# Turning the second norm's rows by DMA from SBUF in place of TensorE transposes, in a one-core decoder kernel

## The chip, the cores and the metric

The kernel runs on one core of a Trainium2 chip, in one launch. The metric is the device time of the run in microseconds (us), the median of several runs. Before the change it is 846.45 us (three runs, 845.71 to 847.24).

## The reference

A decoder layer with three parts, each followed by a layer norm over 512 features; 8 batches of 128 tokens.

```python
x = _layernorm(x + _L0_attn_ref(x, ...))                   # causal self-attention, 32 heads of 16
x = _layernorm(x + _L0_xattn_ref(x, ctx, ctx, mask, ...))  # 32 query heads, 8 key heads of 128, rope
x = _layernorm(x + _L0_ffn_ref(x, ...))                    # gate, up, down; 4-bit weights
# the third part, which reads the output of the second norm:
gate = x2 @ Wg
up = x2 @ Wu
inter = gate * jax.nn.sigmoid(gate) * up
out = (inter @ Wd).astype(jnp.float16)
```

Its inner size is 1376, padded here to 11 tiles of 128. The change concerns the way from the second norm to `x2 @ Wg` and `x2 @ Wu`.

## The kernel before

All 1024 tokens stay in SBUF. `res` holds the running rows: 128 tokens on the partitions, eight batches of 512 features. A product over the features needs the activations turned, with features on the partitions; these are `aTh` and `aTl`, each 128 x 4 x 1024 in fp16. Every fp32 value is split into a high and a low fp16 part, and each product is three matmuls: high by high, low by high, high by low. ScalarE makes the high part (`split_hi`), VectorE subtracts it to get the low part (`split_lo`).

`cTh` and `cTl` hold the turned cross-attention context in the same way. Their last reader is the value projection of the last block of keys and values; after it their room is free until parts of the inner activations are written there.

The program is a row of steps t. From step T0 = 70 on, each step v = t - 70 handles one tile of cross-attention (one batch, four heads), and END = 134. Each engine executes its own list in the order written, and waits on semaphores. For tile v: TensorE makes the scores in step v, VectorE their maximum (`nmax`), ScalarE the exponentials (`prob`) and their sums, VectorE the inverse sums (`rden`), GpSimd the normalised probabilities, ScalarE and GpSimd their two fp16 parts (`pn`). SyncE's DMA queue turns them into `pT` (line 469), and TensorE uses `pT` in step v+2 (`weigh`) and multiplies by the output weights in step v+3 (`merge`). ScalarE and VectorE split the weighed values into `o2h` and `o2l` between these two. "Fills" are projections and turns that TensorE does beside the tiles, by the table of `fill_plan`.

The second norm of batch b is applied when the last head group of that batch is done: in step 127 + b for batches 0 to 3, in step 131 + b for batches 4 to 7 (`APPLY_SLOT`). TensorE then turns the batch: four fp32 transposes of 128 x 128 into a PSUM bank, from which `turned_hi` and `turned_lo` (or `late_turned_hi` and `late_turned_lo`) write `aTh` and `aTl`. Batches 0 to 3 are fills in steps 129, 129, 130 and 131; batches 4 to 7 are turned by `late_turn` in steps 136 to 139.

The first consumer is `gate_or_up`: gate and up for the tiles i = 0 to 3 of the inner size and batches 0 to 3. The first of these (gate, i = 0) stands in step 132, after the scores of tile 62 and ahead of `weigh` of tile 60. The others stand in steps 134 to 138. Then come coded products (`coded_gate_up`, n from 4; lines 1897 and 1898). The second of these, n = 5, is the first that reads batches 4 to 7. The first coded product waits in `bank_free` for `f_inter` to be 3, which is VectorE's product of gate and up for n = 2 (`gated`, line 1438).

SyncE's queue also loads the 4-bit codes and their tables (`load_codes`); from i = 6 on these stand behind the loop over steps.

Of the kernel before, what the change touches and what calls it, by code (L numbers as in the profile page):

```python
# [16 lines left out]
P = 128  # L17
NB, S, D = 8, 128, 512
# [16 lines left out]
E_X = 6  # L35
# [27 lines left out]
def fill_plan():  # L63
# [16 lines left out]
    plan += [(END - 5, "t", (1, 0)), (END - 5, "t", (1, 1)), (END - 4, "t", (1, 2)), (END - 3, "t", (1, 3))]  # L80
# [71 lines left out]
LATE_TURN = {APPLY_SLOT[(1, b)] + 1: b for b in range(BH, NB)}  # L152
# [44 lines left out]
def decoder_kernel(nc, x, xT, ctxT, mask, w1, woT, cols, bo, xwq, xwk, xwv, xwo,  # L197
                   fq, fs, fz, fc, stack_d, tables_d, ident_d, tri_d, cosq_d, sinq_d, cosk_d, sink_d, shq_d, shz_d, out):
    with ExitStack() as ctx:
# [134 lines left out]
        xt_hi, late_psum, late_hi, late_lo = sem("xt_hi"), sem("late_psum"), sem("late_hi"), sem("late_lo")  # L334
# [55 lines left out]
        def by_k(tile):  # L390
            return tile.rearrange("p (k t) -> p k t", k=NK)

# [8 lines left out]
        def _(sp):  # L401
# [69 lines left out]

            def load_codes(i):
# [67 lines left out]
            for t in range(STEPS1 - 8, END + 1):  # L540
                if 1 <= t - T0:
                    turn_probabilities(t - T0 - 1)
                for g in range(2, G):
                    if QKV_SLOT[g - 1][3] + 1 == t:
                        load_q(g)
                    if QKV_SLOT[g - 1][5] + 1 == t:
                        load_kv(g)
                    if OUT_SLOT[g - 1][3] + 1 == t:
                        load_o(g)
                for i, slot in LOAD_CODES.items():  # L550
                    if slot == t:
                        load_codes(i)
            for i in range(len(LOAD_CODES), NI):
                load_codes(i)
# [261 lines left out]
        def _(act):  # L816
# [110 lines left out]
            def late_turned_hi(b):  # L927
                act.wait_ge(late_psum, b - BH + 1)
                split_hi(aTh[:, :, b * S:(b + 1) * S], by_k(bank[4 + b % 2][:, :]), E_X).then_inc(late_hi, 1)
# [187 lines left out]
            for t in range(T0, END + 7):  # L1117
# [29 lines left out]
                if t in LATE_TURN:  # L1147
                    late_turned_hi(LATE_TURN[t])
# [41 lines left out]
        def _(dve):  # L1190
# [87 lines left out]
            def late_turned_lo(b):  # L1278
                dve.wait_ge(late_hi, b - BH + 1)
                split_lo(aTl[:, :, b * S:(b + 1) * S], by_k(bank[4 + b % 2][:, :]), aTh[:, :, b * S:(b + 1) * S],  # L1280
                         E_X).then_inc(late_lo, 1)
# [230 lines left out]
            for t in range(T0, END + 7):  # L1512
# [31 lines left out]
                if t in LATE_TURN:  # L1544
                    late_turned_lo(LATE_TURN[t])
# [94 lines left out]
        def _(pe):  # L1640
# [153 lines left out]
            def late_turn(b):  # L1794
                pe.wait_ge(ln_out, NB + b + 1)
                if b >= BH + 2:
                    pe.wait_ge(late_lo, b - BH - 1)
                elif b == BH:
                    pe.wait_ge(c_o_lo, STEPS - 1)
                else:  # L1800
                    pe.wait_ge(c_o_lo, STEPS)
                for k in range(NK):
                    last = pe_.transpose(bank[4 + b % 2][:, k * P:(k + 1) * P], res[:, b, k * P:(k + 1) * P], ident[:, :])
                last.then_inc(late_psum, 1)

# [42 lines left out]
            def gate_or_up(n, m):  # L1848
                i, half = GATE_UP[n]
                if m == 0:  # L1850
                    pe.wait_ge(f_wlo, i + 1)
                    if n == 0:
                        pe.wait_ge(fill_free, NF)
                    if n == 1:
                        pe.wait_ge(c_exp, STEPS)
                    if n in (2, 3):
                        pe.wait_ge(f_inter, n - 1)
# [30 lines left out]
            def coded_gate_up(n):  # L1888
# [3 lines left out]
                if n == FIRST_LATE:  # L1892
                    pe.wait_ge(late_lo, BH)
# [8 lines left out]
            def down_codes(b):  # L1902
                if b == BH:
                    pe.wait_ge(w_ilo, len(WOVEN))
                if b == 0:
                    pe.wait_ge(f_dcode, len(DOWN_CODES))
                    pe.wait_ge(late_lo, BH)
# [79 lines left out]
            for t in range(T0, END + 7):  # L1987
# [26 lines left out]
                if t in LATE_TURN:  # L2014
                    late_turn(LATE_TURN[t])
# [95 lines left out]
```

## Time and profile before

| | us |
|---|---|
| median of 3 runs | 846.45 (845.71 to 847.24) |
| the profiled execution | 844.59 |
| its span | 842.8 |
| TensorE busy | 826.5 (98%) |
| VectorE busy | 689.8 (82%) |
| GpSimd busy | 641.4 (76%) |
| ScalarE busy | 533.4 (63%) |

The span runs from the first to the last instruction in the profile; the profiled execution's own time is 1.79 us above it. TensorE's granted clock was 0.999 of full speed. Busy shares say which engine has least room on average. What a change is worth is read from the stretch in which it lies, by which wait ends last there. A start time in a timeline is more exact for TensorE than a duration, since matmuls overlap: 0.38 is the length of one, while the next starts 0.22 later.

### The profile page before, as it was taken

The page shows a single profiled execution, that of the slowest core. Times are in us where ns is not written, and L with a number is a line of the kernel's source. Part 1 is how long each engine was busy: PE and PEld are TensorE (multiplying, and loading weights), DVE is VectorE, ACT ScalarE, POOL GpSimd, SP SyncE. Part 2 cuts the span into 40 slices and gives each one's busy share as a digit, 9 for nine tenths or more (in the row PEclk, how much of TensorE's full clock was granted, in tenths as well). Part 3 has the DMA queues.
Part 4 walks back from the last instruction along what each step waited for, and adds up shares of the span by engine and source line. Part 5 has one row for each costly group of instructions (what it writes and reads, how often), then busy time and mean ns, then how long its engine had stood idle before and what let it go on. Part 6 is the DMA issues. An engine that isn't in the chain of part 4 may idle for free.

```text
span 842.8 us, 17394 instructions
## 1 busy us (share of the span) xinstructions
PE 826.5 (98%) x6127; PEld 466.7 (55%) x6127; DVE 689.8 (82%) x1077; ACT 533.4 (63%) x1558; POOL 641.4 (76%) x571
## 2 busy tenths in 40 slices
PE   9999999999999999999999999999999999999997
PEld 4777777665555555555555555555555644434444
DVE  7689788897678778788888888798889756998997
ACT  5898888563866666576675676665666753777400
POOL 2699999996776676578777577578888634899896
PEclk9999999999999999999999999999999999999999
DMA  6675255112253422425325125213432223230011
GB/s 210 232 220 167 76 160 173 34 55 73 39 135 102 109 44 77 101 39 162 89 40 155 34 41 153 38 26 97 130 93 39 46 44 119 63 106 20 2 50 51
DMA packets 113991, 76.77 MB, mean 91 GB/s; under 512 B 71437, under 2 KB 96752, under 8 KB 113904
## 3 DMA queue, kind: packets, MB, share of 16 engines
q1 hardware_dynamic: 112608, 74.34, 32.5%
q10 hardware_dynamic: 1296, 1.32, 0.5%
q8 instruction: 49, 0.80, 0.4%
q14 instruction: 38, 0.31, 0.1%
HBM read 52.50 MB, written 6.36 MB: 70 GB/s over the span
## 4 chain that ended last, share of the span: by engine, by line
PE 66%; POOL 13%; DVE 7%; issue 6%; ACT 5%; DMA 2%; POOLq 0%; ACTq 0%; SPq 0%; DVEq 0%
PE bank L361 17%; PE bank L363 16%; PE bank L362 16%; POOL rot L666 3%; PE bank L1724 3%; POOL q2l L672 2%; POOL pn L683 2%; PE bank L1897 2%; PE bank L1898 2%; POOL prob L676 2%; PE bank L1883 1%; PE bank L1817 1%; PE bank L1816 1%; PE bank L1815 1%; PE bank L1705 1%
## 5 line engine op out<-in xcount | busy, mean ns | idle before, releaser
L676 POOL TENSOR_TENSOR prob<-prob,rden 128x512 f32<-128x512 f32 x64 | 67.8, 1060 | 102.7 <-DVE rden L1355 102.6
L666 POOL TENSOR_TENSOR rot<-rcos,rsin 128x512 f32<-128x512 f32 x80 | 106.5, 1332 | 20.3 <-DVE rsin L1297 19.7
L361 PE MATMUL bank<-aTh,xqh 128*128 128x512 f16 x256 | 97.0, 379 | 2.5 <-DVE rsin L1297 1.5
L361 PE MATMUL bank<-xoh,o2h 128*128 128x512 f16 x256 | 97.0, 379 | 0.1
L362 PE MATMUL bank<-xol,o2h 128*128 128x512 f16 x256 | 97.0, 379 | 0.0
L363 PE MATMUL bank<-xoh,o2l 128*128 128x512 f16 x256 | 97.0, 379 | 0.0
L363 PE MATMUL bank<-aTh,xql 128*128 128x512 f16 x256 | 97.0, 379 | 0.0
L362 PE MATMUL bank<-aTl,xqh 128*128 128x512 f16 x256 | 97.0, 379 | 0.0
L1042 ACT ACTIVATE prob<-bank,ebias 128x128 f32<-128x128 f32 x256 | 90.4, 365 | 2.1
L683 POOL TENSOR_TENSOR pn<-prob,pn 128x512 f16<-128x512 f32 x64 | 84.6, 1322 | 6.6 <-ACT pn L1054 6.4
L1297 DVE SCALAR_TENSOR_TENSOR rsin<-bank,sinq 64x512 f32<-64x512 f32 x128 | 88.1, 688 | 1.7
L672 POOL TENSOR_TENSOR q2l<-rot,q2h 128x512 f16<-128x512 f32 x64 | 81.6, 1275 | 0.0
L912 ACT CAST q2h<-rot 128x512 f16<-128x512 f32 x64 | 39.6, 618 | 61.7 <-POOL rot L666 61.4
L818 ACT ACTIVATE ebias<-nmax 128x4 f32<-128x4 f32 x128 | 26.9, 210 | 76.4 <-DVE nmax L1350 51.1
L867 ACT ACTIVATE prob<-bank,ebias 128x128 f32<-128x128 f32 x256 | 73.0, 368 | 2.1
L1192 DVE SCALAR_TENSOR_TENSOR o2l<-bank,o2h 128x512 f16<-128x512 f32 x64 | 43.6, 681 | 37.0 <-ACT o2h L818 35.8
L1054 ACT CAST pn<-prob 128x512 f16<-128x512 f32 x64 | 39.4, 615 | 52.4 <-POOL prob L676 52.2
L1297 DVE SCALAR_TENSOR_TENSOR rcos<-bank,cosq 128x512 f32<-128x512 f32 x64 | 43.8, 684 | 23.1 <-PE bank L363 23.1
L1216 DVE TENSOR_REDUCE nmax<-bank 128x4 f32<-128x512 f32 x64 | 43.9, 685 | 16.3 <-PE bank L1715 13.5
L1042 ACT ACTIVATION_READ_ACCUMULATOR prob<-bank,ebias 128x1 f32 x256 | 51.9, 203 | 0.0
L1369 DVE SCALAR_TENSOR_TENSOR res<-bank,res 128x512 f32<-128x512 f32 x64 | 43.9, 685 | 8.5 <-PE bank L363 8.2
L1192 DVE SCALAR_TENSOR_TENSOR pT<-bank,pT 128x512 f16<-128x512 f32 x64 | 43.8, 684 | 7.4 <-ACT pT L818 7.1
(234 smaller groups left out, 2661.2 us busy)
## 6 DMA issues: line engine op xcount, KB each, us to landing
tst<-tables SPq DMA_DIRECT2D x11, 768.0 KB, 5.5
xqs<-in_xwq SPq DMA_DIRECT2D x8, 1024.0 KB, 7.2
xos<-in_xwo SPq DMA_DIRECT2D x8, 1024.0 KB, 5.7
qst<-in_fq SPq DMA_DIRECT2D x11, 384.0 KB, 3.4
w1s<-in_w SPq DMA_DIRECT2D x12, 256.0 KB, 5.4
kstk<-stack SPq DMA_DIRECT2D x48, 64.0 KB, 2.3
qstk<-stack SPq DMA_DIRECT2D x21, 128.0 KB, 2.7
xs<-in_ctxT SPq DMA_DIRECT2D x2, 1024.0 KB, 6.9
```

The lines of the kernel that those rows point to most:

```text
L361: pe.matmul(out_ap, ah, bh, start=first, stop=False)
L362: pe.matmul(out_ap, ah, bl, start=False, stop=False)
L363: return pe.matmul(out_ap, al, bh, start=False, stop=last)
L666: nc.gpsimd.tensor_tensor(rot[:, r % 2, :], rcos[:, r % 2, :], rsin[:, r % 2, :], ALU.add).then_inc(rope_rot, 1)
L672: nc.gpsimd.tensor_tensor(lo, rot[:, r % 2, :], hi, ALU.subtract).then_inc(rope_lo, 1)
L676: nc.gpsimd.tensor_tensor(prob[:, v % 2, :].rearrange("p (h k) -> p h k", h=QH), prob[:, v % 2, :].rearrange("p (h k) -> p h k", h=QH), rd ...
L683: nc.gpsimd.tensor_tensor(pn[:, v % 2, 1, :], prob[:, v % 2, :], pn[:, v % 2, 0, :], ALU.subtract).then_inc(c_pn_lo, 1)
L867: last = nc.scalar.activation(prob[:, u % 2, j * S:(j + 1) * S], bank[2 + u % 2][:, j * S:(j + 1) * S], ACT.Exp, bias=ebias[:, u % 2, j:j ...
L1042: last = nc.scalar.activation(prob[:, v % 2, j * S:(j + 1) * S], bank[2 + v % 2][:, j * S:(j + 1) * S], ACT.Exp, bias=ebias[:, v % 2, j:j ...
L1192: return nc.vector.scalar_tensor_tensor(out=dst, in0=src, scalar=2.0 ** e, in1=hi, op0=ALU.mult, op1=ALU.subtract)
L1216: nc.vector.tensor_reduce(nmax[:, u % 2, :], bank[2 + u % 2][:, :].rearrange("p (h k) -> p h k", h=4), AX_X, ALU.max, negate=True).then_in ...
L1297: last = nc.vector.scalar_tensor_tensor(out=as_batches(dst[to, r % 2, :]), in0=as_batches(bank[f % 2][src, :]), scalar=2.0 ** (e - E_X - E_W),
```

## The change

The eight turns of the second norm leave TensorE. In the step in which a batch is normed, ScalarE now writes the high part of the rows of `res` straight into a piece of `cTh`, and VectorE the low part into `cTl` (`late_rows`, tokens on the partitions). In the next step SyncE's queue issues two DMA transposes, `cTh` to `aTh` and `cTl` to `aTl` (`turn_late_rows`). TensorE waits for `rows1_in[0]` at 128, which is both transposes of batches 0 to 3, ahead of the first gate product, and for `rows1_in[1]` at 128 ahead of coded product n = 5. The number of splits stays at eight on each of the two engines, and their source is now SBUF where it was PSUM.

```diff
-    plan += [(END - 5, "t", (1, 0)), (END - 5, "t", (1, 1)), (END - 4, "t", (1, 2)), (END - 3, "t", (1, 3))]
-LATE_TURN = {APPLY_SLOT[(1, b)] + 1: b for b in range(BH, NB)}
+SPLIT_ROWS = {APPLY_SLOT[(1, b)]: b for b in range(NB)}
+        def late_rows(tile, b):
+            return tile[:, b % BH, b // BH * HALF:(b // BH + 1) * HALF]
# SyncE
+            def turn_late_rows(b):
+                for dst, src, done in ((aTh, cTh, rows1_hi), (aTl, cTl, rows1_lo)):
+                    sp.wait_ge(done, b + 1)
+                    sp.dma_start_transpose(dst[:, :, b * S:(b + 1) * S], late_rows(src, b)).then_inc(rows1_in[b // BH], 16)
             for t in range(STEPS1 - 8, END + 1):
                 if 1 <= t - T0:
                     turn_probabilities(t - T0 - 1)
+                if t - 1 in SPLIT_ROWS:
+                    turn_late_rows(SPLIT_ROWS[t - 1])
...
+            for t in range(END, END + 7):
+                if t in SPLIT_ROWS:
+                    turn_late_rows(SPLIT_ROWS[t])
             for i in range(len(LOAD_CODES), NI):
                 load_codes(i)
# ScalarE, at the end of its step
-            def late_turned_hi(b):
-                act.wait_ge(late_psum, b - BH + 1)
-                split_hi(aTh[:, :, b * S:(b + 1) * S], by_k(bank[4 + b % 2][:, :]), E_X).then_inc(late_hi, 1)
+            def late_rows_hi(b):
+                act.wait_ge(ln_out, NB + b + 1)
+                if b % BH == 0:
+                    act.wait_ge(fill_psum, find_fill("v", len(ORDER) - 3 + 2 * (b // BH)) + 1)
+                split_hi(late_rows(cTh, b), res[:, b, :], E_X).then_inc(rows1_hi, 1)
# VectorE, at the end of its step
-            def late_turned_lo(b):
-                dve.wait_ge(late_hi, b - BH + 1)
-                split_lo(aTl[:, :, b * S:(b + 1) * S], by_k(bank[4 + b % 2][:, :]), aTh[:, :, b * S:(b + 1) * S],
-                         E_X).then_inc(late_lo, 1)
+            def late_rows_lo(b):
+                dve.wait_ge(rows1_hi, b + 1)
+                split_lo(late_rows(cTl, b), res[:, b, :], late_rows(cTh, b), E_X).then_inc(rows1_lo, 1)
# TensorE
-            def late_turn(b):
...
                     if n == 0:
                         pe.wait_ge(fill_free, NF)
+                        pe.wait_ge(rows1_in[0], 32 * BH)
...
                 if n == FIRST_LATE:
-                    pe.wait_ge(late_lo, BH)
+                    pe.wait_ge(rows1_in[1], 32 * BH)
```

SyncE's queue before, from the last table load of the attention stage (steps 125 to 137):

```order
L469 DMA_TRANSPOSE pT<-pn 128x8x128 [waits c_pv,c_pn_lo] x10
L480 DMA qst<-in_fq 128x3x512 [waits f_deq]
L482 DMA tst<-tables 128x2x1536
L480 DMA qst<-in_fq 128x3x512 [waits f_deq]
L482 DMA tst<-tables 128x2x1536
L486 DMA wds<-tables 128x512 [waits c_wo]
```

The same queue now, first from tile 60's `pT` on (steps 131 to 135), then its rows from batch 7 on (step 138):

```order
L471 DMA_TRANSPOSE pT<-pn 128x8x128 [waits c_pv,c_pn_lo]
L477 DMA_TRANSPOSE aTh<-cTh 128x4x128 [waits rows1_hi]
L477 DMA_TRANSPOSE aTl<-cTl 128x4x128 [waits rows1_lo]
L471 DMA_TRANSPOSE pT<-pn 128x8x128 [waits c_pv,c_pn_lo] x3
L477 DMA_TRANSPOSE aTh<-cTh 128x4x128 [waits rows1_hi]
L477 DMA_TRANSPOSE aTl<-cTl 128x4x128 [waits rows1_lo]
```

```order
L477 DMA_TRANSPOSE aTh<-cTh 128x4x128 [waits rows1_hi]
L477 DMA_TRANSPOSE aTl<-cTl 128x4x128 [waits rows1_lo]
L487 DMA qst<-in_fq 128x3x512 [waits f_deq]
L489 DMA tst<-tables 128x2x1536
L487 DMA qst<-in_fq 128x3x512 [waits f_deq]
```

The pair that closes batches 0 to 3 stands behind tile 60's `pT`, and the code loads from i = 6 on stand behind batch 7's pair.

TensorE before, the end of tile 62's scores and the first gate product (step 132):

```order
L1815 MATMUL bank<-k2h,q2h 128x128
L1816 MATMUL bank<-k2l,q2h 128x128
L1817 MATMUL bank<-k2h,q2l 128x128
L361 MATMUL bank<-aTh,wgh 128x512 [waits fill_free,f_wlo]
L362 MATMUL bank<-aTl,wgh 128x512
```

The same place now:

```order
L1816 MATMUL bank<-k2h,q2h 128x128
L1817 MATMUL bank<-k2l,q2h 128x128
L1818 MATMUL bank<-k2h,q2l 128x128
L360 MATMUL bank<-aTh,wgh 128x512 [waits rows1_in0,fill_free,f_wlo]
L361 MATMUL bank<-aTl,wgh 128x512
```

The product stands where it stood and has one more wait; `weigh` of tile 60 and all that follows stands behind it.

VectorE before, steps 136 to 139, from the norm of batch 5 on (`res<-res,lnmv,lnrs` is a norm, `res<-bank,res` tile 63's sum into the rows, `gated` the product of gate and up, for n = 2 and then n = 3):

```order
L1262 TENSOR_SCALAR res<-res,lnmv,lnrs 128x512 [waits ln_rs]
L1192 SCALAR_TENSOR_TENSOR aTl<-bank,aTh 128x4x128 [waits late_hi]
L1369 SCALAR_TENSOR_TENSOR res<-bank,res 128x512 [waits c_wo]
L1253 BN_STATS lnst<-res 128x6 [waits c_acc]
L1257 BN_AGGR lnmv<-lnst 128x2 [waits ln_stat]
L1262 TENSOR_SCALAR res<-res,lnmv,lnrs 128x512 [waits ln_rs]
L1192 SCALAR_TENSOR_TENSOR aTl<-bank,aTh 128x4x128 [waits late_hi]
L1262 TENSOR_SCALAR res<-res,lnmv,lnrs 128x512 [waits ln_rs]
L1192 SCALAR_TENSOR_TENSOR aTl<-bank,aTh 128x4x128 [waits late_hi]
L1438 SCALAR_TENSOR_TENSOR gated<-bank,gated 128x512 [waits f_gated,f_up]
L1192 SCALAR_TENSOR_TENSOR aTl<-bank,aTh 128x4x128 [waits late_hi]
L1438 SCALAR_TENSOR_TENSOR gated<-bank,gated 128x512 [waits f_gated,f_up]
```

The same stretch now:

```order
L1276 TENSOR_SCALAR res<-res,lnmv,lnrs 128x512 [waits ln_rs]
L1206 SCALAR_TENSOR_TENSOR cTl<-res,cTh 128x512 [waits rows1_hi]
L1382 SCALAR_TENSOR_TENSOR res<-bank,res 128x512 [waits c_wo]
L1267 BN_STATS lnst<-res 128x6 [waits c_acc]
L1271 BN_AGGR lnmv<-lnst 128x2 [waits ln_stat]
L1276 TENSOR_SCALAR res<-res,lnmv,lnrs 128x512 [waits ln_rs]
L1206 SCALAR_TENSOR_TENSOR cTl<-res,cTh 128x512 [waits rows1_hi]
L1276 TENSOR_SCALAR res<-res,lnmv,lnrs 128x512 [waits ln_rs]
L1206 SCALAR_TENSOR_TENSOR cTl<-res,cTh 128x512 [waits rows1_hi]
L1451 SCALAR_TENSOR_TENSOR gated<-bank,gated 128x512 [waits f_gated,f_up] x2
```

Each low part is now that of the batch whose norm stands right before it. Batch 4's low part has moved ahead of this stretch, and batch 7's ahead of the first `gated`.

## Rows read from the trace of the kernel before

**Rows 1.** The page, busy time and the chain that ended last.
```profile
PE 826.5 (98%) x6127; PEld 466.7 (55%) x6127; DVE 689.8 (82%) x1077; ACT 533.4 (63%) x1558; POOL 641.4 (76%) x571
PE 66%; POOL 13%; DVE 7%; issue 6%; ACT 5%; DMA 2%; POOLq 0%; ACTq 0%; SPq 0%; DVEq 0%
```
**Rows 2.** TensorE in order of time: start us, us, engine, line, what [idle before].
```profile
703.33 0.60 PE L1803 MATMUL bank<-ident,res 128*128 128x128 f32 x4
703.77 0.38 PE L361 MATMUL bank<-aTh,wgh 128*128 128x512 f16 x1
...
706.36 0.60 PE L1803 MATMUL bank<-ident,res 128*128 128x128 f32 x4
707.32 0.66 PE L1803 MATMUL bank<-ident,res 128*128 128x128 f32 x4 [0.36 <-DVE res L1262]
...
713.43 0.38 PE L1897 MATMUL bank<-aTh,dif 128*128 128x512 f16 x1
```
**Rows 3.** TensorE in order of time, steps 131 and 132.
```profile
670.04 0.39 PE L361 MATMUL bank<-pT,v2h 128*128 128x512 f16 x1
...
670.90 0.39 PE L361 MATMUL bank<-xoh,o2h 128*128 128x512 f16 x1
...
674.17 0.38 PE L361 MATMUL bank<-aTh,wgh 128*128 128x512 f16 x1
```
**Rows 4.** SyncE's queue in order of time: tiles 59 and 60.
```profile
666.95 1.23 SPq L469 DMA_TRANSPOSE pT<-pn  x1
672.35 1.23 SPq L469 DMA_TRANSPOSE pT<-pn  x1
```
**Rows 5.** Line 469 over the whole span: issue ns, and time to landing.
```profile
L469 SPq DMA_TRANSPOSE pT<-pn x64: 1232/1232/2128, 215.3 to 686.8; - x64
...
DMA to landing us min/median/max: 3.0/3.0/6.4
```
**Rows 6.** The page's DMA issues: KB each, median us to landing.
```profile
stack<-q1h SPq DMA_DIRECT2D x7, 128.0 KB, 1.8
```
**Rows 7.** ScalarE and VectorE in order of time, steps 130 and 131.
```profile
665.07 0.61 ACT L1054 CAST pn<-prob 128x512 f16<-128x512 f32 x1
...
667.13 0.21 ACT L818 ACTIVATE ebias<-nmax 128x4 f32<-128x4 f32 x1 [0.76 <-DVE nmax L1350]
...
670.15 0.69 DVE L1192 SCALAR_TENSOR_TENSOR o2l<-bank,o2h 128x512 f16<-128x512 f32 x1 [0.83 <-ACT o2h L818]
```
**Rows 8.** Each engine's busy time in a stretch: steps 127 to 129.
```profile
650.00:660.00 10.00, 10.00 (x101) 6.73 (x100) 9.83 (x19) 6.26 (x19) 9.02 (x10) 1.00 0.38 54
```
**Rows 9.** VectorE's low parts (line 1192) by tile: ns min/median/max.
```profile
L1192 DVE SCALAR_TENSOR_TENSOR xql<-xqs,xqh x24: 681/1196/1797, 261.1 to 551.1; 128x512 f16<-128x512 f32 x24
L1192 DVE SCALAR_TENSOR_TENSOR aTl<-bank,aTh x16: 678/682/692, 153.8 to 714.3; 128x512 f16<-128x512 f32 x16
```
**Rows 10.** VectorE and GpSimd in order of time: two norms, and GpSimd's work beside one.
```profile
653.56 1.15 POOL L683 TENSOR_TENSOR pn<-prob,pn 128x512 f16<-128x512 f32 x1
653.84 1.17 DVE L1262 TENSOR_SCALAR res<-res,lnmv,lnrs 128x512 f32<-128x512 f32 x1
...
667.01 0.54 DVE L1262 TENSOR_SCALAR res<-res,lnmv,lnrs 128x512 f32<-128x512 f32 x1
```
**Rows 11.** VectorE and ScalarE in order of time, steps 135 to 138.
```profile
698.98 0.69 DVE L1192 SCALAR_TENSOR_TENSOR o2l<-bank,o2h 128x512 f16<-128x512 f32 x1 [2.11 <-ACT o2h L818]
699.59 0.61 DVE L1394 TENSOR_SCALAR nib<-qst,shq 128x1536 uint16<-128x1536 uint16 x1
...
701.78 0.68 DVE L1369 SCALAR_TENSOR_TENSOR res<-bank,res 128x512 f32<-128x512 f32 x1
702.49 0.69 DVE L1253 BATCH_NORM_STATS2 lnst<-res 128x6 f32<-128x512 f32 x1
...
709.90 0.68 DVE L1438 SCALAR_TENSOR_TENSOR gated<-bank,gated 128x512 f32<-128x512 f32 x1
```
**Rows 12.** The next code loads: the queue's issue, and VectorE's first use.
```profile
695.92 0.48 SPq L482 DMA_DIRECT2D tst<-tables  x1
722.93 0.62 DVE L1394 TENSOR_SCALAR nib<-qst,shq 128x1536 uint16<-128x1536 uint16 x1
tst<-tables SPq DMA_DIRECT2D x11, 768.0 KB, 5.5
```

More of the change, by code:

```diff
@@ L333, in decoder_kernel @@
         ln_shift, ln_mid, ln_right = sem("ln_shift"), sem("ln_mid"), sem("ln_right")
-        xt_hi, late_psum, late_hi, late_lo = sem("xt_hi"), sem("late_psum"), sem("late_hi"), sem("late_lo")
+        xt_hi, rows1_hi, rows1_lo, rows1_in = sem("xt_hi"), sem("rows1_hi"), sem("rows1_lo"), [sem("rows1_in0"), sem("rows1_in1")]
         xq_in, xkv_in, xo_in = sem("xq_in"), sem("xkv_in"), sem("xo_in")
@@ L1146, in _ @@
                     bank_splits([f for f in fills_at(t)[1:] if f not in turned_first(t)])
-                if t in LATE_TURN:
-                    late_turned_hi(LATE_TURN[t])
+                if t in SPLIT_ROWS:
+                    late_rows_hi(SPLIT_ROWS[t])
                 if t == GU_USE[0]:
@@ L1543, in _ @@
                         consume(f)
-                if t in LATE_TURN:
-                    late_turned_lo(LATE_TURN[t])
+                if t in SPLIT_ROWS:
+                    late_rows_lo(SPLIT_ROWS[t])
                 if t == GU_USE[0]:
@@ L1792, in fill @@
                 last.then_inc(fill_psum, 1)
-            def late_turn(b):
[L1795 to L1804, printed above, removed]
             def scores(v):
@@ L1906, in down_codes @@
                     pe.wait_ge(f_dcode, len(DOWN_CODES))
-                    pe.wait_ge(late_lo, BH)
                 for e, k in enumerate(DOWN_CODES):
@@ L2013, in _ @@
                     fill(f)
-                if t in LATE_TURN:
-                    late_turn(LATE_TURN[t])
                 if t in EARLY_GU:
```

## The prediction

> **What bounds the kernel now.** I read the page first: TensorE is busy for 98% of the span and carries 66% of the chain that ended last, with GpSimd 13% and VectorE 7% [rows 1]. So time taken off TensorE counts only where TensorE is not just about to wait for something else. Next came TensorE's timeline around each of the eight turns, and the queues that feed it. Three places differ.
>
> Around 670 us TensorE is paced by the softmax chain. It starts `weigh` of tile 59 at 670.04 [rows 3], which is 3.09 after that tile's `pT` was issued at 666.95 [rows 4], and a `pT` lands 3.0 after its issue [rows 5]. `merge` follows at 670.90 [rows 3], when `o2l`, begun at 670.15, is done [rows 7].
>
> From 670.90 to 706.8 TensorE works without a gap. Whatever delays it there is lost in full.
>
> Between 706.36 and 713.43 the late turns stand on its path, with one wait of 0.36 for a norm [rows 2].
>
> The measure of a turn: four transposes start at 703.33 and the next matmul at 703.77, so 0.44 us a batch and 3.5 us for eight [rows 2]. That is what would be gained if nothing else changed.
>
> **The change part by part.** Times are those of the profiled execution.
>
> *A, the first four turns (steps 129 to 131).* They take 4 x 0.44 = 1.8 us of TensorE. But the chain ends at 670.04 and 670.90 with DMA and VectorE, so TensorE would arrive earlier and wait longer. What counts is how the chain to tile 59's `pT` and to that `merge` moves. Two things pull it forward: ScalarE's `pn` at 665.07 [rows 7] stood behind two high parts that waited for TensorE, of which one remains, without that wait; this is worth up to 0.4. One pushes it back: batches 0 and 1 get their low parts in steps 127 and 128, where VectorE is busy for 9.83 of 10 us and GpSimd for 9.02 [rows 8]. In those steps VectorE has no gap to hide them, so two low parts delay the maxima behind them.
>
> The low part's own price changes too. From PSUM it takes 0.68, never over 0.69. The same operation from SBUF, `xql`, takes 0.68 to 1.80, median 1.20 [rows 9]. What it waits for is seen in a norm, also SBUF to SBUF: 1.17 beside GpSimd's `pn`, which began 0.28 earlier, and 0.54 where GpSimd is idle [rows 10]. The Trainium skill says the same (Advanced Engine Details and Errata, section GPSIMD Details): GpSimd shares a read and a write interface with VectorE, and they conflict when a VectorE instruction has two SBUF inputs; `cTl<-res,cTh` has two, `aTl<-bank,aTh` had one.
>
> Some of this delay is absorbed: the norm that already waits 0.6 for GpSimd then waits less, and `nmax` of tile 60 comes one low part sooner, since step 129 has one where it had two. Following each row through steps 127 to 130 I get the exponentials of tile 60 (before at 667.13 [rows 7]) between 0.3 earlier (low parts at 0.6, their spacing without a wait) and 1.2 later (both at 1.2). I take +0.2, nearer the low end, because the two delays and the two gains nearly cancel. So A is worth nothing: +0.2, from -0.3 to +1.2.
>
> *B, the new wait of the first gate product.* TensorE reaches it at 674.17 [rows 3] and now needs all eight transposes of batches 0 to 3. Batch 3's pair stands in SyncE's queue behind tile 60's `pT`, issued at 672.35 for 1.23 [rows 4]. Its rows are ready at about 671.5, so it is the queue's order that holds it back. Batch 3's splits delay that `pT` by some 0.2. The pair can start at 672.35 + 0.2 + 1.23 = 673.8. The trace has no 128x4x128 transpose. Two of them move what one `pT` moves, so I take one `pT`'s 3.0 to landing and 0.15 for the second issue and the wake-up: 676.95. The wait is 2.8. Lower bound: half of 1.23 to issue the first, then 1.8 for the second, as for a plain copy of 128 KB [rows 6], without the 0.2: 676.0, a wait of 1.8. Upper bound: 1.23 for the first and 3.0 for the second, 678.0 and 3.9. Behind this product in TensorE's order stand `weigh` of tile 60, `merge` of 59 and everything after, and TensorE has no gap until 706.8, so B counts in full: +2.8. ScalarE, VectorE and SyncE follow TensorE again from step 134 on and shift with it.
>
> *C, the last four turns (steps 136 to 139).* Off TensorE go 4 x 0.44 and the gap between 706.80 and 707.32: 1.76 + 0.52 = 2.3. Without B's shift coded product 4 could start at 713.43 - 2.3 = 711.1. It needs `f_inter` 3, the first late `gated`, before at 709.90 [rows 11] and so no limit. Now batch 4's low part stands ahead of the code digits begun at 699.59, and `res` of tile 62 moves from 701.78 to 702.4. Then for batches 5 and 6, each: the sum 0.6, statistics 0.7, aggregate 0.1, norm 0.55, the wait for ScalarE's high part 0.65, low part 0.6, together 3.2. Batch 7's statistics are in these, so it adds norm, wait and low part, 1.8, and `gated` 0.65. Ready: 702.4 + 6.4 + 1.8 + 0.65 = 711.3, a wait of 0.2 at best. GpSimd runs three long operations beside these norms and low parts, which by [rows 10] cost up to 0.5 each; at worst 712.8, a wait of 1.7. I take 1.1, two of three met. C is -2.3 + 1.1 = -1.2, from -2.3 (no wait at all) to -0.6.
>
> *What is hidden.* ScalarE's high parts from SBUF cost what they did. Batch 7's pair lands some 3.2 after its low part at about 711.5, at 714.7; coded product 5 comes 16 matmuls x 0.22 after 712.2, at 715.7: 1.0 to spare. The code loads for i = 6 were issued at 695.92 and are used at 722.93 [rows 12]. Now they are issued at about 712.5 and land at 718.0, against a use at 721.7. If that cover were gone, each us late would be one on VectorE's path. The coded stage and the down products shift unchanged.
>
> *Sum.* +0.2 + 2.8 - 1.2 = +1.8. The profiled execution would go from 844.59 to 846.4. It stood 1.86 under the median, so on the scale of the median: 846.45 + 1.8 = **848.3 us**.
>
> The Trainium skill also has a rule on the choice itself (VectorE: DVE Perf Modes, section The three transpose paths): 390 ns on TensorE against 1309 ns by the DMA crossbar for one 128x128 in 16 bits, and TensorE is advised where PSUM will do. Read as one block after another, batch 3's eight blocks would take 10.5 us, TensorE would wait until 684, and an estimate of 856 follows. The trace speaks against this reading, since a `pT` of eight blocks lands in 3.0; the advice itself it bears out, at 0.11 a block on TensorE.
>
> **The rivals.**
>
> *Not slower.* Batch 3's pair lands as fast as small plain copies do. The place is the wait of the first gate product. Its price is then 1.8, C brings its full 2.3 because GpSimd happens not to stand in VectorE's way, and A brings its 0.3: -0.8, 845.6. It decides where B's wait is no longer than C's gain. For it: the pair's half size. Against: the pair stands behind a `pT` in any case, and VectorE's row of work before `gated` has 0.2 of wait even undisturbed.
>
> *Clearly faster.* The rows of batch 3 are no limit because TensorE arrives late, and the 2.3 of C and a part of A stay: 843.9. Only another order in SyncE's queue would allow it.
>
> *VectorE and GpSimd collide.* Low parts take up to 1.8 in steps 127 to 130 and 135 to 138. A at +1.2, B at 3.9, C at -0.6: +4.5, 850.9. For it: 9.83 and 9.02 busy of 10 [rows 8], and the median of 1.20 [rows 9]. It decides from about 1.1 a low part.
>
> *Batch 7's pair or the code loads come late.* They now stand close together in one queue, and a `pT` has landed as late as 6.4 [rows 5]. Then coded product 5 waits up to 2: 850.3.
>
> **How the numbers follow.** Forecast 0.45, not slower 0.22, clearly faster 0.06, collision 0.17, late landings 0.10. A measurement of this kernel tells 0.2% from no change, 1.7 us: under 844.76 is faster, over 848.14 slower. The forecast's own range, 846.9 to 849.6, lies across the upper edge and I give slower 0.27 of its 0.45; collision and late landings add 0.25, not slower nothing. Slower 0.52. Faster is 0.06 and a little from "not slower": 0.08. Within: 0.40. The range from 845.2 to 850.7 leaves out about one in ten on each side.
>
> **What would show it.** In the changed kernel's profile: the first gate product begins 2 to 4 us after tile 62's scores, waiting for DMA `aTl<-cTl`; `weigh` of tile 59 still starts 3.0 after its `pT`. The first coded product waits for VectorE's `gated` by 0.2 to 1.7; coded product 5 has no wait. `cTl` low parts have a median near 1 us. The prediction is wrong if the first gate product starts within 1 us of the scores, if `merge` of tile 58 starts over 1 us earlier than before, or if the code loads for i = 6 are waited for.

## The result and the profile after

The changed kernel takes 851.16 us (median, 850.54 to 852.33) beside 846.68 before (four runs, 845.71 to 847.24): ratio 1.0059, 95% interval 1.0045 to 1.0072. It is slower by 0.6%. The forecast was 848.3 with a range up to 850.7.

The page of the changed kernel, busy time and the chain, answers [rows 1]:

```profile
PE 823.8 (97%) x6095; PEld 463.3 (55%) x6095; DVE 691.3 (81%) x1077; ACT 533.4 (63%) x1558; POOL 641.9 (76%) x571
PE 60%; POOL 15%; DVE 9%; issue 7%; ACT 6%; DMA 2%; SPq 0%; POOLq 0%; DVEq 0%; ACTq 0%
```

TensorE has less work (826.5 before) in a span 5.9 us longer, so it waits more. The list of its waits between 600 and 760 us says for what (line and tile, then total, times, longest):

```profile
PE bank L1899 <- DVE gated L1451: 2.7, 1, 2.7
PE bank L360 <- DMA aTl<-cTl: 2.7, 1, 2.7
PE bank L360 <- DMA pT<-pn: 2.3, 2, 2.1
```

Its timeline around these, in the columns of [rows 2]: `weigh` of tile 59, the first gate product, the first coded product with the two matmuls behind it, and the first product of the next gate and up, woven between coded ones (from here on "the first woven product").

```profile
671.37 0.39 PE L360 MATMUL bank<-pT,v2h 128*128 128x512 f16 x1 [2.05 <-DMA pT<-pn]
...
678.16 0.38 PE L360 MATMUL bank<-aTh,wgh 128*128 128x512 f16 x1 [2.71 <-DMA aTl<-cTl]
...
717.97 0.58 PE L1899 MATMUL bank<-aTh,dif 128*128 128x512 f16 x1 [2.72 <-DVE gated L1451]
718.35 0.63 PE L1900 MATMUL bank<-aTl,dif 128*128 128x512 f16 x1
718.78 0.64 PE L1899 MATMUL bank<-aTh,dif 128*128 128x512 f16 x1
...
723.47 0.38 PE L1885 MATMUL bank<-aTh,wgh 128*128 128x512 f16 x1
```

Read against before, with one correction: the chance waits of the first 150 us differ from one execution to the next, and this execution entered the stretch 0.42 late (`weigh` of tile 57 at 660.26, before at 659.84). I take such a start off every shift and call the rest the local shift. The two rows of before that this needs and that [rows 2] and [rows 3] do not have:

```profile
659.84 0.38 PE L361 MATMUL bank<-pT,v2h 128*128 128x512 f16 x1
...
717.66 0.38 PE L1883 MATMUL bank<-aTh,wgh 128*128 128x512 f16 x1
```

- First gate product: 678.16 against 674.17 [rows 3], +3.99, locally **+3.57**. It stays so until the first late turn, at 703.33 before.
- First coded product: 717.97 against 713.43 [rows 2], +4.54, locally +4.12. So the late turns brought **+0.55** where they should have brought time: 2.33 gained (the four turns and the gap; the rounded 4 x 0.44 + 0.52 of [rows 2] give 2.28), a wait of 0.55 + 2.33 = 2.88 added. The profile calls 2.72 of it idle.
- First woven product: 723.47 against 717.66, +5.81, locally +5.39. Another **+1.27** has come in, without a wait. The coded matmuls start 0.43 apart instead of 0.22, for eight matmuls.

The table of windows shows this last part (window, length, TensorE busy, granted clock, DMA share, GB/s): the first 3.0 and 2.9 us behind the two waits.

```profile
717.90:720.90 3.00, 2.93 (x7) 0.50 0.53 105
678.10:681.00 2.90, 2.84 (x14) 1.00 0.48 90
```

At the start of the coded stage TensorE ran at 0.50 of full clock, 1.2 of 2.4 GHz; after the equally long wait at 678 it ran at full clock.

The queue of SyncE around the first gate product, as in [rows 4]:

```profile
667.38 1.23 SPq L471 DMA_TRANSPOSE pT<-pn  x1
...
672.93 1.23 SPq L471 DMA_TRANSPOSE pT<-pn  x1
674.20 1.28 SPq L477 DMA_TRANSPOSE aTh<-cTh  x1
675.53 1.27 SPq L477 DMA_TRANSPOSE aTl<-cTl  x1
```

The new transposes, which answers [rows 5]: the issue of the low parts' (ns), then the time to landing of all 16.

```profile
L477 SPq DMA_TRANSPOSE aTl<-cTl x8: 1188/1264/1270, 658.2 to 718.0; - x8
...
DMA to landing us min/median/max: 2.4/2.5/3.2
```

Batch 3's pair begins at 674.20, or 673.78 with the start taken off, where the forecast had 673.8. But the second issue starts 1.33 later, not 0.15, and lands 2.63 after that: 678.16.

And VectorE from `res` of tile 62 to the late `gated`, as in [rows 11], the high parts that it waits for named in brackets:

```profile
706.37 0.68 DVE L1382 SCALAR_TENSOR_TENSOR res<-bank,res 128x512 f32<-128x512 f32 x1
...
707.91 0.72 DVE L1276 TENSOR_SCALAR res<-res,lnmv,lnrs 128x512 f32<-128x512 f32 x1
709.33 1.70 DVE L1206 SCALAR_TENSOR_TENSOR cTl<-res,cTh 128x512 f16<-128x512 f32 x1 [0.70 <-ACT cTh L830]
710.95 0.68 DVE L1382 SCALAR_TENSOR_TENSOR res<-bank,res 128x512 f32<-128x512 f32 x1
...
713.70 1.68 DVE L1206 SCALAR_TENSOR_TENSOR cTl<-res,cTh 128x512 f16<-128x512 f32 x1 [0.70 <-ACT cTh L830]
715.30 0.54 DVE L1276 TENSOR_SCALAR res<-res,lnmv,lnrs 128x512 f32<-128x512 f32 x1
716.53 0.69 DVE L1206 SCALAR_TENSOR_TENSOR cTl<-res,cTh 128x512 f16<-128x512 f32 x1 [0.70 <-ACT cTh L830]
717.14 0.68 DVE L1451 SCALAR_TENSOR_TENSOR gated<-bank,gated 128x512 f32<-128x512 f32 x1
```

GpSimd in the same stretch, the two operations that lie beside low parts (`wdl` is the low part of decoded down weights):

```profile
709.32 1.16 POOL L728 TENSOR_TENSOR wdl<-deq,wdh 128x512 f16<-128x512 f32 x1
713.68 1.15 POOL L728 TENSOR_TENSOR wdl<-deq,wdh 128x512 f16<-128x512 f32 x1
```

Two of the three low parts of `cTl` take 1.70 and 1.68. Beside each, begun within 0.02 us, stands a `wdl` of GpSimd. The third, with GpSimd idle, takes 0.69. Each is also preceded by 0.70 of waiting for ScalarE's high part.

### The profile page after: what moved, and what is told of

The parts are those of the page before. It is cut to its first block, busy times and chain, and to the rows that moved or that the text cites. A ratio compares the mean times of both kernels' runs of the same rounds, so it can differ in the third digit from the quotient of the medians.

```text
span 848.7 us, 17339 instructions
## 1 busy us (share of the span) xinstructions
PE 823.8 (97%) x6095; PEld 463.3 (55%) x6095; DVE 691.3 (81%) x1077; ACT 533.4 (63%) x1558; POOL 641.9 (76%) x571
## 4 chain that ended last, share of the span: by engine, by line
PE 60%; POOL 15%; DVE 9%; issue 7%; ACT 6%; DMA 2%; SPq 0%; POOLq 0%; DVEq 0%; ACTq 0%
PE bank L360 16%; PE bank L362 15%; PE bank L361 15%; POOL rot L678 3%; PE bank L1737 2%; POOL pn L695 2%; POOL q2l L684 2%; POOL left L711 2%; POOL prob L688 2%; ACT prob L879 1%; DVE total L1438 1%; PE bank L1899 1%; ACT prob L1056 1%; PE bank L1900 1%; PE bank L1818 1%
```

## The experiments

My theory after this comparison: three causes add up. The order of SyncE's queue fixes the first gate product; VectorE's row of work (with the waits for ScalarE, and low parts stretched by GpSimd) fixes the first coded product; and a long TensorE wait can be followed by a stretch at half clock. The rivals stand with each run. Ratios are to the kernel before on the same chip, with 95% intervals. The local shift is that of the first woven product in the profile, start taken off.

| kernel | median us | ratio | wait, first gate product | wait, first coded product | stretches at half clock | local shift |
|---|---|---|---|---|---|---|
| changed | 851.16 | 1.0059 (1.0045 to 1.0072) | 2.71 | 2.72 | second wait | +5.39 |
| changed, again | 852.38 | 1.0070 (1.0057 to 1.0082) | 3.38 | 2.73 | both | +6.89 |
| only batches 0 to 3 by DMA | 851.70 | 1.0056 (1.0036 to 1.0075) | 3.39 | none new | first | +5.26 |
| only batches 4 to 7 by DMA | 846.93 | 1.0003 (0.9989 to 1.0018) | none | 1.72 | none | -0.52 |
| batch 3's pair before `pT` | 848.93 | 1.0019 (1.0006 to 1.0032) | 1.29 | 2.72 | second | +3.36 |
| the same, again | 848.07 | 1.0021 (1.0007 to 1.0035) | 0.46 | 2.73 | none | +0.92 |
| late splits a step later | 848.98 | 1.0028 (1.0015 to 1.0040) | 3.38 | none | first | +3.32 |
| changed, matmuls in the wait | 851.45 | 1.0059 (1.0045 to 1.0073) | 3.40 | filled | first | +5.44 |
| changed, GpSimd moved | 852.09 | 1.0061 (1.0048 to 1.0074) | 3.38 | 0.73 | first | +5.08 |
| pair first, splits later | 845.30 | 0.9986 (0.9977 to 0.9996) | 1.56 | none | none | -0.21 |
| late only, splits later | 843.98 | 0.9974 (0.9964 to 0.9985) | none | none | none | -1.00 |
| pair first, matmuls in the wait | 847.69 | 1.0020 (1.0011 to 1.0029) | 1.63 | filled | none | +2.12 |
| batches 4 to 6 only, splits later | 844.32 | 0.9978 (0.9968 to 0.9987) | none | none | none | -1.89 |

For "GpSimd moved" the shift is read behind a further wait (below), at the second woven product; at the first it was +3.54. Local shift and ratio agree to within 1.8 us, so a single profile tells the mechanism, and the times tell its worth.

### Only batches 0 to 3 by DMA

```diff
-SPLIT_ROWS = {APPLY_SLOT[(1, b)]: b for b in range(NB)}
+SPLIT_ROWS = {APPLY_SLOT[(1, b)]: b for b in range(BH)}
+LATE_TURN = {APPLY_SLOT[(1, b)] + 1: b for b in range(BH, NB)}
...
```

> Only batches 0 to 3 go through DMA transposes; batches 4 to 7 are turned on TensorE from their finished rows as before. Theory (the order of SyncE's queue): the first gate product keeps its wait of 2.7 to 2.9 for the transposes of batch 3, and TensorE keeps the whole shift of 3.6 (0.7 by the softmax chain, 2.9 by the wait) to the end, since it has no gap behind it: 846.7 + 3.5 = 850.2, and no wait of the first coded product beyond the 0.4 of before. Rival (VectorE and GpSimd collide, and the late stage is what costs): most of the 4.5 lies in the late stage, so this kernel stands at about 847.7 (+1).

Measured: +5.2 us by the medians. The rival (+1) falls: the early half alone costs as much as the whole change did. My 3.5 was too small as well. TensorE waits 3.39 here, and the 12 matmuls behind the wait take 4.27 (678.72 to 682.99) where before they took 2.59. The window of them (columns as above):

```profile
678.70:682.90 4.20, 4.18 (x12) 0.60 0.33 62
```

So the half clock comes here too, and costs 1.68 us: 3.58 + 1.68 = 5.26, the shift at the end.

### Only batches 4 to 7 by DMA

```diff
+    plan += [(END - 5, "t", (1, 0)), (END - 5, "t", (1, 1)), (END - 4, "t", (1, 2)), (END - 3, "t", (1, 3))]
-SPLIT_ROWS = {APPLY_SLOT[(1, b)]: b for b in range(NB)}
+SPLIT_ROWS = {APPLY_SLOT[(1, b)]: b for b in range(BH, NB)}
...
```

> Only batches 4 to 7 go through DMA transposes; batches 0 to 3 are turned on TensorE as fills as before. Theory: no wait of the first gate product; the first coded product waits for VectorE's gated by 2.5 to 3, which takes back the 2.3 that the turns off TensorE give, +0.5; and if the half clock behind that wait comes again it adds 1.3. So 847.2 to 848.5, against 846.7 before. Forecast's own reading (wait of 1.1): 845.5. If the half clock came from TensorE's earlier wait at the first gate product as well, the granted clock behind the coded wait is 1.0 here and the time 847.2.

Measured: no difference that the interval shows. The wait for `gated` is 1.72, one microsecond less than expected: of the two low parts that stood beside a `wdl`, one now starts just ahead of it, and then the `wdl` is the one that is stretched. VectorE there:

```profile
707.79 0.69 DVE L1207 SCALAR_TENSOR_TENSOR cTl<-res,cTh 128x512 f16<-128x512 f32 x1 [0.69 <-ACT cTh L831]
```

And GpSimd:

```profile
707.80 1.71 POOL L729 TENSOR_TENSOR wdl<-deq,wdh 128x512 f16<-128x512 f32 x1
```

In these three pairs only one of two operations begun together pays, VectorE's 1.0 or GpSimd's 0.55, and it is the one that began 0.01 to 0.02 us later. In this profile there is no half clock behind the wait of 1.72.

### Batch 3's pair ahead of tile 60's `pT`

```diff
+                if SPLIT_ROWS.get(t - 1) == BH - 1:
+                    turn_late_rows(BH - 1)
                 if 1 <= t - T0:
                     turn_probabilities(t - T0 - 1)
-                if t - 1 in SPLIT_ROWS:
+                if t - 1 in SPLIT_ROWS and SPLIT_ROWS[t - 1] != BH - 1:
                     turn_late_rows(SPLIT_ROWS[t - 1])
```

> As the changed kernel, but SyncE issues batch 3's pair of transposes ahead of tile 60's pT instead of behind it. Theory (the queue's order holds the pair back): the pair is issued some 1.3 to 2.5 earlier, the first gate product waits 0 to 0.6 instead of 2.7, and tile 60's pT, needed only behind 24 gate and up products of 512 columns, is late by 2.6 without being waited for: -2.3 against the changed kernel, 848.8. Rival (the landing of the pair is what lasts, whatever stands before it; or VectorE's low part of batch 3 is late): wait of 2 or more stays, under -1.

Expected 848.8, measured 848.93. The second measurement of the same kernel:

> Batch 3's pair ahead of tile 60's pT once more, as the base for the kernel with the dummy matmuls on the same chip: 848.9, wait of the first gate product 1.3 at clock 1.0, wait for gated 2.7 and eight coded matmuls at 0.43.

848.07, and the two ratios agree (1.0019, 1.0021). The wait fell to 1.29 (0 to 0.6 expected) and 0.46 (1.3 expected), so the queue's order is the cause and the landing is not. The eight coded matmuls at 0.43 that I expected again did not come, though the wait for `gated` was 2.73: the matmuls behind it start 0.22 apart.

```profile
714.97 0.38 PE L1901 MATMUL bank<-aTh,dif 128*128 128x512 f16 x1 [2.73 <-DVE gated L1453]
715.19 0.38 PE L1902 MATMUL bank<-aTl,dif 128*128 128x512 f16 x1
```

The waits of the first gate product differ because the first transpose of the pair was issued in 2.08 in one execution and 1.27 in the other. The queue of the first:

```profile
671.00 1.27 SPq L477 DMA_TRANSPOSE aTl<-cTl  x1
672.32 2.08 SPq L477 DMA_TRANSPOSE aTh<-cTh  x1
674.45 1.27 SPq L477 DMA_TRANSPOSE aTl<-cTl  x1
```

And of the second:

```profile
669.90 1.27 SPq L477 DMA_TRANSPOSE aTl<-cTl  x1
671.21 1.27 SPq L477 DMA_TRANSPOSE aTh<-cTh  x1
672.52 1.27 SPq L477 DMA_TRANSPOSE aTl<-cTl  x1
```

The pair now starts when batch 2's pair has been issued, not when its rows are ready: five transposes at 1.3 fill the queue. The two other kernels with the pair first had a long issue at the same place, 2.37 and 2.45, and waits of 1.56 and 1.63: in all four profiles the wait is 0.46 plus what this issue took above 1.27, to 0.02. What lengthens it is not shown.

### The splits of batches 4 to 7 a step later

```diff
-SPLIT_ROWS = {APPLY_SLOT[(1, b)]: b for b in range(NB)}
+SPLIT_ROWS = {APPLY_SLOT[(1, b)] + b // BH: b for b in range(NB)}
```

> As the changed kernel, but the splits of batches 4 to 7 stand one step later in ScalarE's and VectorE's order, so VectorE doesn't wait for ScalarE's high part after each norm and gated(2) stands ahead of batch 7's splits. Theory (VectorE's row of norm, wait for ScalarE, low part is what makes the first coded product late): the wait of 2.7 for gated falls under 0.5, the half clock behind it goes with it (1.3), together -3.5 to -4: 847.2. Batch 7's pair then lands later and coded product 5 may wait up to 1. Rival (each low part of 1.7 beside GpSimd is the cost): the low parts meet GpSimd's operations in the new place as well, and only about 1.2 to 1.5 comes back: 849.8.

Measured 848.98, between the theory's 847.2 and the rival's 849.8. The mechanism is as expected: the waits for ScalarE's high parts of batches 4 to 6 are gone, those low parts take 0.68, `gated` stands ahead of batch 7's low part, and TensorE goes from gate products to coded ones without a gap. Coded product 5 then waits 0.6. But this execution also has the 3.38 wait and the half clock at 678, which the first profile of the changed kernel had not. Against the second profile, which had both, the local shift is 3.6 less (6.89 to 3.32), the size that the theory gave; by the ratios (1.0059 and 1.0070 to 1.0028) it is 2.6 to 3.6.

### Matmuls in the wait

```diff
+                if c == 0:
+                    for _ in range(12):
+                        pe_.matmul(bank[WOVEN_BANK[0]][:, :], aTh[:, 0, 0:P], aTh[:, 0, 0:HALF], start=True, stop=True)
```

> As the changed kernel, plus 12 matmuls of 512 columns between the last gate product and the first coded product, into a bank that the next product overwrites (more work, the same output). They fill the 2.7 to 2.9 in which TensorE waits for gated. Theory (the half clock in the first coded matmuls comes from TensorE standing idle for 2.7 or more): the granted clock stays at 1.0 (2.4 GHz) at the start of the coded stage, the coded matmuls are spaced 0.22 from the first, and the kernel gains 1.3 on the changed kernel: 849.9. Rival (the half clock belongs to the place, to the coded matmuls or the transfers beside them, not to the wait): spacing of 0.43 for the first eight stays, time unchanged at 851.2.

The clock part holds. The window of 3 us from the first coded matmul:

```profile
721.60:724.60 3.00, 2.99 (x14) 1.00 0.58 96
```

Full clock, against 0.50 before. The time did not move: 851.45. The profile is 1.45 locally below the second profile of the changed kernel and level with the first, since the half clock at 678 came in this one. I repeated the test with the same three lines on the kernel that has batch 3's pair first, where the first wait is short.

> Batch 3's pair ahead of tile 60's pT, and the 12 dummy matmuls ahead of the first coded product. With the first gate wait at 1.3 the half clock is there once only, behind the wait for gated. Theory (it comes of the idle time and costs 1.3): granted clock 1.0 at the start of the coded stage and 1.3 less than the same kernel without dummies: 847.6. Rival (the half clock hides behind something else that is late, since the first of these tests moved the clock and not the time): the clock rises and the time stays at 848.9.

847.69 against 848.07 and 848.93 without the matmuls; the ratio, 1.0020 against 1.0021 and 1.0019, did not move. What the times can't settle, the granted clock of each execution tells in part. Without the matmuls, 13 of 24 executions of this kernel had a mean clock of 0.996 or 0.997, median time 849.1; the other 11 had 0.998 or more, median 846.9. With the matmuls all 12 had 0.998 or more. So the matmuls do keep the clock up, and the half clock does not come in every execution. That the filling saves time is not shown; 13 in 24 times 1.5 us is 0.8, within the intervals.

### The changed kernel again, unaltered

> The changed kernel once more, unaltered: the first profile of it had tile 59's pT landing 3.9 after its issue, a wait of 2.7 at the first gate product and no half clock behind it, while four kernels with the same order there had 3.3, a wait of 3.4 and the half clock (4.27 instead of 2.59 for 12 matmuls). Theory A (which of the two comes is chance in that pT's landing): this profile shows 1.3, 3.4 and the half clock, local shift behind it 5.2 instead of 3.6, time 851 to 853. Theory B (it belongs to the kernel): 2.1, 2.7 and clock 1.0 again, 851.2.

Theory A: the waits are 3.38 and 2.73. Its two windows, behind the first and behind the second wait:

```profile
678.60:683.00 4.40, 4.34 (x13) 0.61 0.32 60
719.90:722.90 3.00, 2.73 (x7) 0.50 0.50 95
```

The first gate product starts at the same place as in the first profile, start taken off (678.66 - 0.93 = 677.73; 678.16 - 0.42 = 677.74). SyncE's queue sets it. What varies is when TensorE gets there: tile 59's `pT` was waited for until 3.32 after its issue in this execution and until 3.99 in the first, so the wait was 3.38 instead of 2.71, and the clock fell. The earlier arrival gained nothing and the half clock cost 1.7 us. The nine executions of the two measurements fall in two groups, 850.5 to 851.5 with a mean clock of 0.997 or 0.998, and 852.1 to 852.6 with 0.995.

### GpSimd off the low parts

```diff
-                    if DOWN_EARLY[i] + 1 == t:
+                    if DOWN_EARLY[i] + 4 == t:
                         down_lo(i)
```

> As the changed kernel, but GpSimd's operations wdl of the code pieces 4 and 5 stand three steps later in its order, away from VectorE's low parts of batches 5 and 6. Theory (a low part that reads SBUF costs 1.70 beside GpSimd's wdl and 0.68 alone): both low parts take 0.68, gated comes 2.0 earlier, the wait of the first coded product falls from 2.7 to about 0.7, and the half clock behind it goes: -2.0 - 1.3 = -3.3, 847.9. Rival (something else that GpSimd does, or the queue of VectorE alone, stretches the low parts): low parts stay over 1.2, gain under 1.

VectorE's two low parts, with no `wdl` beside them:

```profile
710.98 0.69 DVE L1206 SCALAR_TENSOR_TENSOR cTl<-res,cTh 128x512 f16<-128x512 f32 x1 [0.70 <-ACT cTh L830]
...
714.34 0.69 DVE L1206 SCALAR_TENSOR_TENSOR cTl<-res,cTh 128x512 f16<-128x512 f32 x1 [0.69 <-ACT cTh L830]
```

The prediction of the mechanism was met to 0.03: 1.70 became 0.69, the wait for `gated` 0.73, and the half clock behind it went. The time was not met, 852.09 where I expected 847.9. Part of it is a new wait:

```profile
PE bank L1899 <- DVE total L1438: 1.1, 1, 1.1
PE bank L1899 <- DVE gated L1451: 0.7, 1, 0.7
```

The two `wdl`, 2.27 together, now stand ahead of the partial sums `left` that `total` needs. This takes back 1.5 (the local shift goes from 3.54 to 5.08). Part is the half clock at 678, present here. Locally the kernel is still 1.8 below the second profile of the changed kernel. Its ratio, 1.0061, lies between the changed kernel's two, 1.0059 and 1.0070, and each is known to some 1.1 us, so the times do not show that the move gained anything. That the stretched low parts made `gated` late is shown by the profile; what they cost in time is not shown by this run.

### Pair first and splits later, together

The two edits shown above, in one kernel.

> Both reorderings on the changed kernel: batch 3's pair ahead of tile 60's pT, and the splits of batches 4 to 7 a step later. Theory: the terms add up. Against before: A 0, the wait of the first gate product +1.4, C -2.3 with 0.5 of new waiting at coded product 5: -0.4, 846.1, and no stretch at half clock. Rival (with the first wait smaller, VectorE's row falls behind again and the wait for gated comes back): 1 to 2 more, 847.5.

845.30, a little faster than before (0.9986, interval up to 0.9996), where the terms gave -0.4. The rival falls: neither wait is long, and its profile shows no half clock. By the ratios the two reorderings together are worth 6.2 us of the changed kernel (1.0059 to 0.9986), the pair first by itself 3.3 (to 1.0020), the later splits 2.6 (to 1.0028): the parts add up within their intervals. Coded product 5 waits 0.57 here.

### Only the late batches, with later splits

```diff
+    plan += [(END - 5, "t", (1, 0)), (END - 5, "t", (1, 1)), (END - 4, "t", (1, 2)), (END - 3, "t", (1, 3))]
+SPLIT_ROWS = {APPLY_SLOT[(1, b)] + 1: b for b in range(BH, NB)}
...
```

> Batches 0 to 3 turned on TensorE as before, batches 4 to 7 by DMA with their splits a step later. Theory: the only gain of the change (2.3 of TensorE time in steps 136 to 139) comes through, less about 0.6 for coded product 5, which waits for batch 7's pair: -1.7, 844.8. Rival (the wait for gated of 1.7 seen with the late batches alone stays, since TensorE is 3 earlier here than with the early waits): -0.5, 846.0.

843.98, ratio 0.9974: the lowest of all, and 0.26% faster than before. The rival falls, since the first coded product waits for nothing. In its profile coded product 5 waited 1.7 for batch 7's pair, whose first issue took 2.13:

```profile
713.53 2.13 SPq L478 DMA_TRANSPOSE aTh<-cTh  x1
716.00 1.20 SPq L478 DMA_TRANSPOSE aTl<-cTl  x1
```

So I gave batch 7 back to TensorE, where it stands as before:

```diff
+SPLIT_ROWS = {APPLY_SLOT[(1, b)] + 1: b for b in range(BH, NB - 1)}
+LATE_TURN = {APPLY_SLOT[(1, NB - 1)] + 1: NB - 1}
...
```

> Batches 4 to 6 by DMA with their splits a step later; batches 0 to 3 and batch 7 turned on TensorE as before. Theory: the wait of 1.7 of coded product 5 for batch 7's pair goes, and a turn of 0.44 comes: 1.3 less than with all four late batches by DMA (844.0), 842.7, or -1.9 by the terms against before (844.8). Rival (batch 7's turn waits for its norm, or its low part stands where gated needs VectorE, so the wait comes back in product 4): 844 to 845, no gain over the four.

The timeline is the sum of its terms: the turn, the first coded product, and the first woven one.

```profile
710.90 0.60 PE L1827 MATMUL bank<-ident,res 128*128 128x128 f32 x4
711.34 0.38 PE L1922 MATMUL bank<-aTh,dif 128*128 128x512 f16 x1
...
715.57 0.38 PE L1907 MATMUL bank<-aTh,wgh 128*128 128x512 f16 x1
```

Start taken off, the coded product is 1.89 earlier than before, which is 2.33 less one turn of 0.44; measured 844.32, 1.9 less than 846.19, as the terms gave. The 842.7 expected from the four batches was not met: it does not beat the version with four batches by DMA (0.9978 against 0.9974, intervals overlapping), so the wait of 1.7 in that one's profile is not shown to cost anything in the times. Whether it was a rare one stays open. The rival's "no gain over the four" came, by the times, but not its mechanism: the profile has no wait at product 4. Both beat both kernels of this case.

## Why the prediction was wrong, step by step

The sum had +1.8; the profile's local shift is +5.39 and the ratio gives 5.0 us. Of the 3.6 that the sum missed in the profile, 0.57 lies in A and B, 1.75 in C, and 1.27 is the half clock.

**The first gate product (A and B).** Right in mechanism, a little small: 3.0 forecast for both, 3.57 measured. A could not be separated from B by its cost: the queue fixes the product's time, and A only decides how long the wait looks, so adding A's 0.2 to a B counted up to 676.95 counted it twice. The share of A was 0.7 and 0.0 in the two profiles (forecast 0.2), by how late tile 59's `pT` landed. B's start (673.8) was met to 0.02. The product, forecast at 676.95, came at 677.74, and these 0.79 lie in taking 0.15 for the second issue: a transpose of half the size takes as long to issue as a whole `pT`, 1.33 from one to the next, 1.18 more. The landing, 2.63 in place of 3.0, gives 0.37 back. The upper bound, 3.9, had the mechanism right. Moving the pair ahead of the `pT` took off 3.3 by the ratios (1.0059 to 1.0020), so the queue's order is the cause.

**C is the step that failed.** It said "C is -2.3 + 1.1 = -1.2, from -2.3 to -0.6"; it was +0.55, since the wait was 2.9. The start of the row was right: `res` of tile 62 at 702.4 forecast, 706.37 less 3.99 = 702.38 measured. The row behind it was not. For batch 5, sum 0.71, statistics 0.73, aggregate 0.10, norm 0.72, wait for ScalarE 0.70, low part 1.62 to the next start: 4.58; for batch 6 4.35. The forecast had 3.2 for each. Of the 2.5 us of excess 2.0 are the two low parts, priced at 0.6, for which an allowance of 0.9 for GpSimd ("up to 0.5 each") stood in the sum. And [rows 9] already showed 1.20 as the median and 1.80 as the most of the same operation from SBUF. I had used those rows for the early steps and the milder norm of [rows 10] for the late ones. With GpSimd moved off, the low parts took 0.69; with the splits a step later the wait was gone. The Trainium skill says that GpSimd shares a read and a write interface with VectorE, and that they conflict when a VectorE instruction has two SBUF inputs (Advanced Engine Details and Errata, section GPSIMD Details). The traces agree: 1.70 beside a `wdl` against 0.69 without, 1.0 us more.

**The half clock was in no term.** It cost 1.3 behind the second wait and, where the first wait reached 3.4, 1.7 behind that. Every window that I read of the kernel before had full clock (two of its 80 executions beside these runs, not profiled, had a mean of 0.996), and the sum treated each wait as costing its own length. What brings the half clock is not settled: filling the wait kept the clock up, but one wait of 2.71 and one of 2.73 had none behind them.

**The rivals.** The collision was the nearest in time (850.9), and its mechanism is a part of what happened. That its number came so near is luck, since its terms were others: it put the price into A and B, where the queue was the limit, and kept C at -0.6. Late landings of batch 7's pair (850.3) did not come: coded product 5 did not wait in the changed kernel. Clearly faster, by another order in the queue, is where the experiments ended, though the queue alone was not enough.

**What was hidden** stayed hidden: no code load was waited for, and ScalarE's high parts took 0.62 to 0.63. Of the signs, the wait of the first gate product (2 to 4 us) and the absence of one at coded product 5 came as forecast; the wait for `gated` was 2.7 where 0.2 to 1.7 was given.

## What to carry to other kernels

Before moving work off the busiest engine, list what its successor waits for in each place. Here only 0.52 of gap and four turns on the path could be gained, 2.3 us, and the two new waits cost more. Price an operation by the worst row of its own kind that has the same neighbour, not by a milder one of another kind. When the wait can't be avoided, put the transfers that something is about to wait for ahead of those needed later, and let the splits trail by a step, so that no in-order engine stands waiting for another after each piece.

## What the runs showed of the hardware

- A DMA transpose of 128x4x128 is issued in 1.19 to 1.29 us, a `pT` of twice the size in 1.23; landing takes 2.5 (median) against 3.0 to 3.1. In 6 of the 13 profiles with such transposes one issue took 1.9 to 2.5, each time with another transpose just ahead of it in the queue.
- A VectorE low part with two SBUF inputs takes 0.68 alone and 1.70 when a GpSimd `wdl` began 0.01 to 0.02 us ahead of it. If it began 0.01 us before GpSimd, GpSimd's took 1.71 in place of 1.16, and VectorE's 0.69.
- Of the first gate and first coded products, TensorE's granted clock fell to 0.50 (1.2 GHz) behind every wait of 3.38 to 3.40 (five profiles of five), behind three of four waits of 2.72 or 2.73, and behind none of 2.71 (one) or of up to 1.72. It cost 1.1 to 1.7 each time against the same matmuls of before. Of two waits of 2.7 in one execution one had it and one had not, so the length alone does not decide.
- The Trainium skill advises a 128x128 transpose on TensorE where PSUM will do as destination (VectorE: DVE Perf Modes, section Rules for kernel authors). It held for the first four batches, which alone by DMA cost about 5 us. It did not hold for the last: with three or four late batches by DMA and their splits a step later the kernel is 1.9 to 2.2 us faster than with none.
